# Two attention prologues of a four-layer cross-attention stack: key transposes, projections and rotations in another order

## The reference, cut to what matters

```python
    x = x + jnp.tanh(g_xattn[1]) * _L1_xattn_ref(_layernorm(x, axis=-1), ctx_4096, ctx_4096, L1_xattn_Wq, L1_xattn_Wk, L1_xattn_Wv, L1_xattn_Wd)
    ...
    x = x + jnp.tanh(g_xattn[3]) * _L3_xattn_ref(_layernorm(x, axis=-1), ctx_4096, mask_1x1xSxS2_ff0, L3_xattn_Wq, L3_xattn_Wk, L3_xattn_Wv, L3_xattn_Wo, L3_xattn_q_norm_w, L3_xattn_k_norm_w)
```

```python
    # second layer
        queries = _rope(queries)
        keys = _rope(keys)
        scores = jnp.einsum('bhqd,bhkd->bhqk', queries, keys) * scale
        scores = jnp.where(causal[None, None], scores, jnp.finfo(scores.dtype).min)
        attn = jax.nn.softmax(scores, axis=-1)
        ctx = jnp.einsum('bhqk,bhkd->bhqd', attn, values)
        return ctx @ Wd.T
    # fourth layer
        q = _rmsnorm(q, q_norm_w)
        k = _rmsnorm(k, k_norm_w)
        scores = jnp.einsum('bhqd,bhkd->bhqk', q, k) * scale
        scores = scores + attention_mask[:, :, :, :kv_len]
        probs = jax.nn.softmax(scores.astype(jnp.float32), axis=-1).astype(q.dtype)
        out = jnp.einsum('bhqk,bhkd->bhqd', probs, v)
        return out @ Wo.T
```

## Time and profile before

| what | value |
|---|---|
| median of 3 runs | 2027.99 us (2025.11, 2027.99, 2036.49) |
| the profiled execution's own time | 2028.37 us |
| its span on the core | 2026.6 us |
| mean granted TensorE clock | 0.975 |
| TensorE busy | 1910.8 us, 94% of the span |
| VectorE, ScalarE, GpSimd busy | 1392.4, 1061.5, 928.2 us |

### The profile page before, as it was taken

The page is one execution under the profiler, slowest core; times in us unless marked ns, Lnnn a source line. Parts: engine busy times, 40 slices in busy tenths (PEclk is TensorE's granted clock), DMA queues, the critical chain, the costliest instruction groups (busy, mean ns, idle before and its releaser), DMA issues.

```text
span 2026.6 us, 33785 instructions
## 1 busy us (share of the span) xinstructions
PE 1910.8 (94%) x11138; PEld 1635.6 (81%) x11138; DVE 1392.4 (69%) x2507; ACT 1061.5 (52%) x2413; POOL 928.2 (46%) x998
## 2 busy tenths in 40 slices
PE   6999999999779999998999999998799999999998
PEld 5888888888658888886767888887588889888986
DVE  5777777767778888887235656656576667667665
ACT  4776767767444545542125455542265555556552
POOL 3654655645556566653323232232254444445432
PEclk9999999999979999999989999998799999999999
DMA  4222222221311121121210010001110111011101
GB/s 149 85 58 81 84 73 88 65 68 58 105 42 63 53 67 52 58 72 30 73 57 14 27 34 6 32 2 48 57 53 12 47 48 47 17 47 48 37 1 49
DMA packets 47774, 106.79 MB, mean 53 GB/s; under 512 B 6128, under 2 KB 19952, under 8 KB 44192
## 3 DMA queue, kind: packets, MB, share of 16 engines
q1 hardware_dynamic: 47648, 105.14, 16.3%
HBM read 98.37 MB, written 6.75 MB: 52 GB/s over the span
## 4 chain that ended last, share of the span: by engine, by line
PE 84%; DVE 9%; issue 3%; ACT 2%; POOL 1%; DMA 0%; DVEq 0%; ACTq 0%; POOLq 0%
PE psX L429 28%; PE psQ L429 15%; PE psO L429 14%; PE psS L429 12%; PE psT L913 7%; PE psSX L429 3%; PE psT L429 2%; PE psX L1010 1%; DVE p_sb L1116 1%; DVE nbias L1120 1%; DVE pT_lo L1132 1%; DVE xn_f L567 1%; DVE qscr L1092 1%; DVE ln_stat L557 1%; PE psS L610 1%
## 5 line engine op out<-in xcount | busy, mean ns | idle before, releaser
L1557 POOL TENSOR_SCALAR p_sb<-p_sb,rrec 128x512 f32<-128x512 f32 (+1 forms) x288 | 233.8, 812 | 493.9 <-DVE rrec L1128 493.9
L1386 ACT ACTIVATE pT_hi<-psT 128x512 fp32r<-128x512 f32 (+2 forms) x384 | 234.9, 612 | 306.7 <-PE psT L913 306.1
L1132 DVE TENSOR_TENSOR pT_lo<-psT,pT_hi 128x512 fp32r<-128x512 f32 (+2 forms) x384 | 271.2, 706 | 63.2 <-ACT pT_hi L1386 62.5
L429 PE MATMUL psO<-pT_hi,v_hi 128*128 128x256 f32 (+1 forms) x832 | 253.4, 305 | 18.0 <-DVE pT_lo L1132 16.3
L429 PE MATMUL psO<-pT_lo,v_hi 128*128 128x256 f32 (+1 forms) x832 | 235.1, 283 | 0.0
L429 PE MATMUL psO<-pT_hi,v_lo 128*128 128x256 f32 (+1 forms) x832 | 235.0, 282 | 0.0
L913 PE MATMUL psT<-ident,p_sb 128*128 128x128 f32 x1408 | 212.9, 274 | 10.7 <-POOL p_sb L1557 7.2
L913 PEld LDWEIGHTS psT<-ident,p_sb 128*128 128x128 f32 x1408 | 172.4, 141 | 49.6 <-POOL p_sb L1557 9.8
L429 PE MATMUL psQ<-xnT_hi,wq_hi 128*128 128x512 f32 x428 | 180.3, 421 | 9.9 <-DVE xnT_lo L589 4.2
L429 PEld LDWEIGHTS psO<-pT_hi,v_hi 128*128 128x128 f32 (+1 forms) x832 | 153.3, 184 | 25.2 <-DVE pT_lo L1132 20.9
L429 PE MATMUL psQ<-xnT_hi,wq_lo 128*128 128x512 f32 x428 | 172.6, 403 | 0.0
(11 more groups left out here) (484 smaller groups left out, 5102.1 us busy)
## 6 DMA issues: line engine op xcount, KB each, us to landing
wq_f<-in_a_wq SPq DMA_DIRECT2D x108, 256.0 KB, 2.7
wo_f<-in_a_wo SPq DMA_DIRECT2D x24, 1024.0 KB, 4.9
wkv_f<-in_a_wkv SPq DMA_DIRECT2D x16, 512.0 KB, 3.7
mask_sb<-in_codes SPq DMA_DIRECT2D x32, 174.0 KB, 2.4
qscr<-in_amax SPq DMA_DIRECT2D x32, 174.0 KB, 2.3
w<-qscr SPq DMA_DIRECT2D x32, 174.0 KB, 1.9
wo_f<-in_f_wT SPq DMA_DIRECT2D x3, 1024.0 KB, 4.9
wo_f<-in_a_wo SPq DMA_DIRECT2D x4, 768.0 KB, 4.4
```

What stands on the lines that cost most here:

```text
L429: mm = pe.matmul(dst, w, m, start=(first and k == 0), stop=(last and k == n - 1))
L1132: L.t_lo.inc(dve.tensor_tensor(pT_view(L, pT_lo, j), t_view(L, j), pT_view(L, pT_hi, j).bitcast(F32), ALU.subtract))
L1386: L.t_hi.inc(act.activation(pT_view(L, pT_hi, j), t_view(L, j), ACT.Copy))
L1557: L.s_norm.inc(pool.tensor_scalar(p_view(L, j), p_view(L, j), rrec[:, j:j + 1], 1.0, ALU.mult, ALU.mult))
```

## The change

In the fourth layer TensorE now issues both key transposes between the norm's transposes and the wait for the norm's last lo part (`ready` becomes 2). Query 1 goes to the bank `psO` as in the second layer, right behind query 0, and query 2 follows the first two scores in the prologue; its place in head 0 is dropped (`started`). ScalarE and VectorE take the key parts first. The first product with the values now also waits until query 1 has been read from `psO`.

In the second layer TensorE's order stays. Query 1 is rotated into the free buffer `xn_f` instead of `qscr`, right behind `q_low` of query 0 and ahead of the row maxima; ScalarE rounds it ahead of the exponentials, VectorE makes its lo part ahead of the values' lo part (`t0`).

```diff
-        self.early, self.ready = ((0, 0), (2, 2), (0, 1), (0, 0))[index]
+        self.early, self.ready = ((0, 0), (2, 2), (0, 1), (0, 2))[index]
...
-            return psO if L.rope and g.loop is None and (g.off, h) == (0, 1) else psQ
+            return psO if L.masked and g.loop is None and (g.off, h) == (0, 1) else psQ
+
+        def q_turned(g, h):
+            return xn_f if g.loop is None and (g.off, h) == (0, 1) else qscr
```

TensorE's parts, in `q_proj`, `weighted_v`, the prologue and `head`:

```diff
-                if L.rope and not started and h < 3:
-                    L.q_f.wait(pe, h - 1)
+                if L.masked and not started and h < 3:
+                    (L.q_f if L.rope else L.q_lo).wait(pe, h - 1)
...
-                    if L.rope and g.loop is None and (g.off, h) == (0, 0):
-                        L.q_f.wait(pe, 2)
+                    if L.masked and g.loop is None and (g.off, h) == (0, 0):
+                        (L.q_f if L.rope else L.q_lo).wait(pe, 2)
...
-                if L.rope:
+                if L.masked:
                     q_proj(Group(0), 1)
                 for u in L.first[L.ready:L.split]:
-                    if L.rms and u == "k1":
-                        q_proj(Group(0), 1)
                     use(None, u, Group(0))
...
-                if L.pairs:
+                if L.masked:
                     q_proj(Group(0), 2)
...
-                    if j == L.q_slot(g, h) and L.query(g, h, L.q_lead):
+                    started = not L.rms or g.loop is not None or g.off or h
+                    if j == L.q_slot(g, h) and L.query(g, h, L.q_lead) and started:
                         q_proj(*L.query(g, h, L.q_lead))
```

VectorE's prologue:

```diff
+                if L.rms:
+                    for u in L.first[:L.split]:
+                        use(None, u, Group(0))
                 q_low(Group(0), 0)
                 if L.rope:
-                    use(None, "t0", Group(0))
+                    q_front(Group(0), 1)
                     for j in range(L.ahead):
                         row_max(Group(0), 0, j)
-                    q_front(Group(0), 1)
+                    q_low(Group(0), 1)
+                    use(None, "t0", Group(0))
                     for j in range(L.settle):
                         row_recip(Group(0), 0, j)
-                    q_low(Group(0), 1)
                 elif L.rms:
-                    for u in L.first:
+                    for u in L.first[L.split:]:
                         use(None, u, Group(0))
```

ScalarE's prologue:

```diff
+                if L.rms:
+                    for u in L.first[:L.split]:
+                        use(None, u, Group(0))
                 q_high(Group(0), 0)
                 w_high(act, L, "wq", Group(0), 2)
                 if L.rope:
                     use(None, "t0", Group(0))
+                    q_high(Group(0), 1)
                     for j in range(L.ahead):
                         row_exp(Group(0), 0, j)
-                    q_high(Group(0), 1)
                     w_high(act, L, "wq", Group(0), 3)
                     return
```

21 lines of the change are left out of this document (12 added, 9 removed).

## The result

The changed kernel takes **2014.16 us** (median of 6 runs, 2012.77 to 2018.79), the kernel before, run beside it, 2027.06 us (6 runs, 2025.11 to 2036.49). The ratio is 0.9939, 95% interval 0.9925 to 0.9954: 12.9 us less between the medians, 12.4 by the ratio. The profiled execution took 2013.30 us.

The account below looks back on a forecast made before the run. TensorE, busy 94% of the span, was taken to bound the kernel. Gains of 8.0 + 3.2 less 2.6 and 0.8 made 7.8 us off 2028.37: 2020.6, stated as 2020.5 us, range 2015.0 to 2026.5.

Parts of the forecast that it names:

- The mask: Fourth layer: ScalarE's first key part now waits for the mask's transfer, covered by 5.6 us of slack.
- The fourth layer's give-back: A low clock stretch behind TensorE's idle 2.8 us before the second product with the values; costs 2.6 us.
- The clock gives some back: New idle gaps bring low clock, costing 2.6 us (fourth layer) and 0.8 (second); key transposes could not raise it earlier.
- Rival A: All gains arrive: no new clock drop, 11.2 us, or transposes also raise it earlier, 12.9; 2017 to 2015.5 us; chance 0.22.
- the second layer's give-back: A low clock stretch behind an idle gap of 2.4 us before the second product with the values; costs 0.8 us.
- the third line: Span from the second layer's second product with the values to the fourth layer's first projection; predicted 0.8 us longer.
- the gain from the waits: TensorE's waits removed or shortened: gross 8.0 us in the fourth layer and 3.2 us in the second.
- B: Head 0 without filler: fourth layer's low clock 7.0 us longer, second layer's wait only shifts; net 4 us, 2024.4; chance 0.20.
- C: Fourth layer, from the second product with the values: low clock holds 33 us more, slower at 2033.7 us; chance 0.05.
- D: Fourth layer: third query's projection waits for something else ahead of the scores, gain lost; 2025 to 2028 us; chance 0.03.

Follow-up runs that it names:

- experiment 8: The changed kernel with six matmuls of 128x512 added in the fourth layer's gap before the transposes of head 1's first slot; ratio 0.9934 to the kernel before.
- experiment 4: The kernel before with eight more key transposes, results overwritten, ahead of the fourth layer's wait for the norm's last lo part; 0.9992, 2025.14 us.
- experiment 5: The kernel before with four single-column products ahead of the fourth layer's wait for the norm's last lo part; run once, 2023.45 us.
- experiment 3: The changed kernel with the fourth layer's eight key transposes behind query 0's projection, not ahead of it; 0.996 of the kernel before, 2018.13 us.
- experiment 11: The changed kernel with six filler matmuls in the fourth layer's gap and query 3's weight parts made earlier in the second layer; 0.9942, 2014.84 us.

## Why the prediction was wrong

**What held.** The paths, and the reading of the profile but for two rows on the clock. The first projection starts 0.06 us behind the lo part it waits for (1431.57; lo part at 1430.82 with 0.69). Query 1 follows it at once. The row maximum comes 1.36 us behind the scale (predicted 1.35), the first transposes 3.88 us behind the row maximum, with 0.35 us of waiting (0.4), and 8.94 us behind the start of query 1's projection (9.1). Query 2's lo part comes 9.70 us behind the first row maximum (10.1), and the second product with the values 5.20 us behind that (5.2). From the end of the first projection 8.4 us are gone, predicted 8.0; in the second layer 3.2 and 3.2. The mask cost nothing. The fourth layer's give-back came behind the place that I had named, the gap before head 1's first slot (experiment 8), and was larger: 3.65 us to the last mark, predicted 2.6. One of the two rows is read wrongly there. The clock fell at 1453.9, so the stretch of the earlier trace rows with 1.45 us of work lay already in the low time; ahead of the fall TensorE was busy 1.73 of 3.40 us. The low stretch lasted 10.2 us, of which I had counted 7.0.

**The step that failed** is in "The clock gives some back": "That stretch of 3.40 us decides whether the key transposes, now ahead of the first projection, could also let the clock rise earlier; it says they could not." The stretch from 1457.0 to 1460.4 held a sum of squares of single columns, three score matmuls and four transposes. I laid its low clock on the transposes, and it could not decide that. Experiments 4 and 5 put the two kinds apart in one place: behind transposes the clock is at 1.00, behind single columns at 0.50. So the first projection ran at the high clock and 2.45 us fell away that I had priced at nothing. Rival A has 1.7 us for an earlier rise (12.9 against 11.2), and no run shows that figure. Before, the whole projection lay at the low clock, which rose only at 1443.7; in the traces without such transposes it took 4.35 to 5.49 us, so in its place the early rise is worth 1.3 to 2.5. How much of that reaches the end is not shown. Experiment 3 goes without the early rise, has no low stretch further on, and is no later at the last mark; experiment 4 has the rise, falls again, and is level with experiment 5.

**The second term mis-sized** is the second layer's give-back: 0.8 us predicted, none there. I had one gap of 2.4 us before its second product. The wait for the weights, which I had missed, put query 3's projection 0.9 us later than in my working (593.25 and the 2.15 us of earlier start make 595.4, against 594.5) and so split the gap: 1.48 us before the projection, 1.29 before the product. The clock stayed at 1.00 through both, where it was at 0.51 in the earlier trace rows. The change rather took low stretches away: between 588 and 620 us the four traces with the second layer as before have one or two each; of the nine with it changed, six have none. The missed wait itself cost nothing that experiment 11 could find; query 3's rotation came when I had it, at VectorE's turn.

**The rest** of the difference between the two spans lies in shared code: 2.0 us ahead of the second layer and 1.6 behind the last mark. That is luck of this pair of traces, and it lets them look better than the ratio: 15.1 us against 12.4 by the timed runs. Without it 11.5 us are left. That lies inside the interval of the timed ratio (9.3 to 15.2 us); from the 7.8 us predicted to it go the failed step with 2.45, the third line with 1.8 (0.8 of give-back predicted, 1.0 of gain found) and the waits with 0.4, and the fourth layer's larger give-back takes 1.05 of that back. From the timed median before, 2027.06 us, the 11.5 us would lead to 2015.6, just inside my range, so what the traces name does not settle the last 1.4 us down to 2014.16.

**The rivals.** A came nearest, by its second branch: the transposes counted, and nearly all of the gain from the waits arrived. I named 2015.5 for it; measured 2014.16. But A had no give-back, and that did come in the fourth layer. So its number is near in part by luck. B's condition, low clock for longer, did not come, nor did C's: the clock was back at 1461.8. D is excluded by the timeline. The range failed at its low end because it took A's 12.9 us as the most there could be and left nothing for the low stretches that come and go in other places, each about 1.7 us by my estimate.

**What stays open.** How the fourth layer's gain divides between its edits. Keys ahead and query 2 behind the scores each bring most alone by the traces, but the timed intervals overlap, and single traces depend on where the clock's steps fall. With the keys ahead, moving query 2 saves 2.4 us in its place, and the traces show none of it at the last mark; the timed 1.8 us is within the noise. That single columns don't bring the clock up rests on one trace, and so does what a step that falls earlier among the transposes does.

## What to carry to other kernels

Where TensorE waits for a small tail behind transposes, put other ready work there. Here it was eight key transposes of 128x128 in a wait of 1.41 us: the projection still started 0.06 us behind the lo part that it waits for, and in seven of eight traces it came up at the high clock, worth 1.3 to 2.5 us in its place. Single columns in that wait left it at the low clock in one trace (4.41 us), and behind three products of 128x512 ahead of the second layer's projection the first matmul still took 0.79 us in another. Look for gaps further on as well: in experiment 4 the clock fell again at 1441.0, behind a wait of 1.83 us, and to the last mark it was level with experiment 5 (533.0 and 532.9 us). Before a stretch of the trace is taken as proof that a kind of work does not raise the clock, list what the stretch holds; if it holds two suspects, it decides neither. And a filler moved out of one gap to close another leaves a gap behind: count the low stretches on both sides, since local gains of 2.4 us came to almost nothing here. Before distances to the end of a trace are compared, look where the low stretches behind the last changed place lie: they made up to 4 us here.

## What the runs showed of the hardware

- Transposes of 128x128 can bring the clock up: 3.16 us of them within 3.40, and the next stretch is at 1.00 (experiment 4; the same in six of the seven other traces with transposes there). Products with a single column did not, in one trace: 3.05 us of transposes and such columns, and the next 3.40 us are at 0.50, although TensorE was busy for all of them.
- Waits of 1.69 or 1.70 and 0.41 us were followed by 6.8 us at the low clock in three traces; with six matmuls, 1.53 us in all, in the first of them the clock stayed up in two traces, and the last mark came 2.7 to 4.0 us earlier (524.4 and 523.6 against 527.0 to 527.6). In experiment 3 the same waits were followed by no fall.
- Low stretches move between places of code that no edit touched (at 71.6 us in two of the 13 traces, at 1750.4 in one). In two executions of the changed kernel they lie ahead of the second layer at 543.7 and 564.1 us, and at 520.2 and 568.0. A single trace is then off by about 1.7 us for each 3.4 us, an estimate from the two clock levels and from 0.43 us between the starts of two 128x512 products at 0.50 against 0.23 at 1.00.
- TensorE took its work in the written order: in the kernel before, the second four key transposes wait only for `early_free`, yet started at 1448.42, behind the projection that had waited 1.59 us for `q_lo`. In the new order all eight start at 1429.95.
